# Rank-major place numbers with one load per unit, and overflow sums in bank 7 with three buffers of V

## The reference, cut to what matters

```python
h = relu(layernorm(x)); row, col = edge_index             # 6250 nodes, 206250 edges, float32
m = concatenate([h[col], edge_attr], axis=1)
m = relu(m @ W1.T + b1)
m = relu(m @ W2.T + b2)
summed = segment_sum(m, row, num_segments=6250)           # row = src, col = dst (sorted)
agg = summed / maximum(segment_sum(ones, row), 1)[:, None]
z = relu(concatenate([h, agg, u[batch]], axis=1) @ Wa.T + ba)
out = x + z @ Wb.T + bb
```

## Time and profile before

| | us |
|---|---|
| median of 3 runs | 1899.47 (1896.35 to 1899.72) |
| the profiled execution | 1902.48 |
| its span, first to last instruction | 1900.7 |
| first and last start of an indirect transfer on GpSimd | 69.6 and 1834.7 |

### The profile page before, as it was taken

The page is one execution under the profiler, slowest core; times in us unless marked ns, Lnnn a source line. Parts: engine busy times, 40 slices in busy tenths (PEclk is TensorE's granted clock), DMA queues, the critical chain, the costliest instruction groups (busy, mean ns, idle before and its releaser), DMA issues.

```text
span 1900.7 us, 43131 instructions
## 1 busy us (share of the span) xinstructions
PE 1732.0 (91%) x12376; PEld 1463.0 (77%) x12376; DVE 1340.0 (71%) x4868; ACT 1428.0 (75%) x2591; POOL 1509.7 (79%) x991
## 2 busy tenths in 40 slices
PE   5898888999999999999899999999999999976828
PEld 3676777888888888888788888888888888866725
DVE  8665655777777777778677777777777777755727
ACT  4687877888888888888788888888888888842315
POOL 8488888888888888888888888888888888878850
PEclk9999999999999999999999999999999999988968
DMA  9988888999999999999899999999999999997755
GB/s 330 269 169 145 156 148 141 199 197 205 195 207 187 199 203 199 194 205 197 176 199 194 199 202 200 195 194 209 202 191 201 200 204 202 199 210 155 159 136 198
DMA packets 312201, 369.10 MB, mean 194 GB/s; under 512 B 40832, under 2 KB 196064, under 8 KB 311328
## 3 DMA queue, kind: packets, MB, share of 16 engines
q1 hardware_dynamic: 175200, 302.12, 55.1%
q0 software_dynamic: 135360, 62.15, 34.5%
q10 hardware_dynamic: 1408, 2.03, 0.3%
HBM read 203.87 MB, written 159.27 MB: 191 GB/s over the span
## 4 chain that ended last, share of the span: by engine, by line
POOL 53%; issue 20%; DMA 11%; PE 9%; ACT 3%; DVE 2%; SPq 1%; POOLq 0%; ACTq 0%; DVEq 0%
POOL sums L819 48%; DMA sums<-regA,idx 9%; POOL sums L807 5%; PE bank L1351 2%; PE bank L1400 2%; PE bank L1362 1%; DMA sums<-vscat,vidx 1%; PE bank L1374 1%; ACT h L921 1%; PE bank L1390 1%; ACT regA L929 1%; PE bank L1276 1%; PE bank L1476 1%; ACT regA L955 0%; DMA p_table<-regB 0%
## 5 line engine op out<-in xcount | busy, mean ns | idle before, releaser
L819 POOL DMA_INDIRECT sums<-regA,idx x844 | 1318.3, 1562 | 293.0 <-issue 242.6
L1351 PEld LDWEIGHTS bank<-h,regC 128*128 128x128 f32 x3072 | 387.4, 193 | 180.7 <-ACT h L940 127.8
L1351 PE MATMUL bank<-h,regC 128*128 128x130 f32 x3072 | 432.0, 284 | 64.5 <-ACT h L940 64.5
L1374 PE MATMUL bank<-regA,L 128*128 128x512 f32 x806 | 432.3, 619 | 2.8 <-DVE regA L1143 2.7
L1400 PE MATMUL bank<-w,h 128*128 128x128 f32 x3224 | 430.1, 277 | 0.0
L1400 PEld LDWEIGHTS bank<-w,h 128*128 128x128 f32 x3224 | 396.8, 194 | 1.1 <-ACT h L921 0.6
L921 ACT ACTIVATE h<-bank,b1c 128x512 f32<-128x512 f32 x403 | 275.6, 684 | 136.9 <-PE bank L1374 131.9
L1362 PE MATMUL bank<-regC 128*128 128x129 f32 x2352 | 296.9, 280 | 23.0 <-DVE regB L1130 12.7
L1390 PEld LDWEIGHTS bank<-h,regC 128*128 128x128 f32 x1688 | 218.9, 191 | 119.7 <-issue 91.3
L1362 PEld LDWEIGHTS bank<-regC 128*128 128x128 f32 x2352 | 277.4, 194 | 37.3 <-ACT vscat L961 21.9
L904 ACT ACTIVATE regC<-bank 128x520 f32<-128x520 f32 x384 | 231.8, 604 | 87.8 <-PE bank L1351 84.5
(11 more groups left out here) (143 smaller groups left out, 1526.9 us busy)
## 6 DMA issues: line engine op xcount, KB each, us to landing
regC<-slots SPq DMA_DIRECT2D x294, 260.0 KB, 5.6
regA<-in_ea SPq DMA_DIRECT2D x202, 256.0 KB
slots<-regC SPq DMA_DIRECT2D x192, 260.0 KB
src<-rows_src SPq DMA_DIRECT2D x107, 256.0 KB
slots<-regC SPq DMA_DIRECT2D x192, 138.1 KB
sums<-regA,idx POOLq DMA_INDIRECT x844
dstR<-rows_dst SPq DMA_DIRECT2D x101, 128.0 KB
sums<-zeros SPq DMA_DIRECT2D x20, 645.0 KB, 6.7
```

Of the source, the lines that this page charges most:

```text
L819: nc.gpsimd.indirect_dma_start(out=sums[k], out_offset=bass.IndirectOffsetOnAxis(ap=idx[:, n % RING, t:t + 1], axis=0), in_=scat[:, n % 4, ...
L1351: last = T.matmul(psSlot(t)[:, k, :], place, h2[:, g % 2, t, :], start=True, stop=True)
L1374: T.matmul(psL1(s % 2), L[:, s % RING, :], R[:, s % RING, :], start=True, stop=True).then_inc(l1_done, 1)
```

## The change

Places are numbered rank by rank instead of bin by bin: place `j * 49 + b` is rank `j` of bin `b`, before it was `4 * b + j`. The permutation is built with its two inner loops exchanged (same 784 elements). The two bins of a unit now lie beside each other in `slots` for each rank, so that one DMA of 128 partitions with 4160 contiguous bytes replaces two with 2080 each. `arrived` counts one landing per load.

The overflow sums move from bank 1 to columns 260 to 388 of bank 7, beside the plain sums. V gets three buffers, and the waits before its first half is written are loosened by one pair. `VSUM` becomes 9 and `VLAG` 8: TensorE sums V in the step after, ahead of the plain sums of the same step, behind `free_sums`, and without the waits of L1422 and L1423; the unit's wait of L1426 goes; a wait for the overflow copy enters `free_sums` of a plain group, ahead of the next group's sums. ScalarE copies the overflow sums right behind the plain sums, not at the end of the step. GpSimd issues L807 three steps later, between two plain groups. With `VSUM` the last block's units shift: four instead of three of them run one to a step, and the last comes one step later.

```diff
-QLAG, VPRE, VREAD, VBC, VMASK, VSUM, VLAG = 6, 3, 7, 6, 7, 8, 5
+QLAG, VPRE, VREAD, VBC, VMASK, VSUM, VLAG = 6, 3, 7, 6, 7, 9, 8
 def arrived(m):
-    parts = {n: unit_bins(q)[1] for (_, q), n in UNIT_NO.items()}
-    return sum(parts[n] for n in users(m))
+    return len(users(m))
-        V = sb("V", [P, 2, W], f32)
+        V = sb("V", [P, 3, W], f32)
-        psVsum = bank[:, 1, PAIR * C:(PAIR + 1) * C]
+        psVsum = bank[:, 7, 2 * W:2 * W + C]
@@ sync: the unit's load
-                    for i in range(nb):
-                        sp.dma_start(loaded(m)[0:CAP * len(block), i, :, :].rearrange("p t c -> p (t c)"),
-                                     slots[h0:h0 + len(block), CAP * (b + i):CAP * (b + i + 1), :]).then_inc(unit_in[buffer_of(m)], 16)
+                    side_by_side = slots[h0:h0 + len(block), :, :].rearrange("n (j b) x -> (n j) (b x)", b=NBIN)
+                    sp.dma_start(loaded(m)[0:CAP * len(block), 0:nb, :, :].rearrange("p b t c -> p (b t c)"),
+                                 side_by_side[:, b * TPG * W:(b + nb) * TPG * W]).then_inc(unit_in[buffer_of(m)], 16)
@@ scalar: these lines move from the end of the step to behind the copy of the plain sums
+                if closes(s - VSUM):
+                    j = BINNED_NO[s - VSUM] // 2
+                    act.wait_ge(vsum_done, j + 1)
+                    if j >= 4:
+                        landed(act, BINNED[2 * (j - 4) + 1], 0)
+                    nc.scalar.activation(vscat[:, j % 4, :], psVsum, ACT.Copy).then_inc(vscat_ready, 1)
@@ vector
-                    VE.tensor_tensor(perm[:, n % 2, :, OVER:PW].rearrange("p t (b j) -> p t b j", j=CAP), ranked.unsqueeze(3).broadcast_to([P, TPG, NBIN, CAP]),
-                                     ranks[:, :].unsqueeze(1).unsqueeze(1).broadcast_to([P, TPG, NBIN, CAP]), ALU.is_equal).then_inc(perm_ready, 1)
+                    VE.tensor_tensor(perm[:, n % 2, :, OVER:PW].rearrange("p t (j b) -> p t j b", b=NBIN), ranked.unsqueeze(2).broadcast_to([P, TPG, CAP, NBIN]),
+                                     ranks[:, :].unsqueeze(1).unsqueeze(3).broadcast_to([P, TPG, CAP, NBIN]), ALU.is_equal).then_inc(perm_ready, 1)
-                        wait(dve, vsum_done, j - 1)
-                        wait(dve, vidx_ready, j - 1)
+                        wait(dve, vsum_done, j - 2)
+                        wait(dve, vidx_ready, j - 2)
@@ tensor: free_sums, and the sum of V ahead of the plain sums
                     pe.wait_ge(scat_ready, PLAIN_NO[g] + 1)
+                    wait(pe, vscat_ready, sum(1 for q in BINNED if closes(q) and q + VSUM <= g + 2))
+                if closes(s - VSUM):
+                    j = BINNED_NO[s - VSUM] // 2
+                    pe.wait_ge(vmask_ready, j + 1)
+                    free_sums(min(g - 1, NG - 1))
+                    T.matmul(psVsum, vS[:, j % 2, :] if not general else zeros[:, 0:P], V[:, j % 3, 0:C], start=True, stop=True).then_inc(vsum_done, 1)
-                if closes(s - VSUM):
-                    j = BINNED_NO[s - VSUM] // 2
-                    pe.wait_ge(vmask_ready, j + 1)
-                    wait(pe, vscat_ready, j)
-                    wait(pe, acc_ready, units_until(s - 1))
-                    T.matmul(psVsum, vS[:, j % 2, :] if not general else zeros[:, 0:P], V[:, j % 2, 0:C], start=True, stop=True).then_inc(vsum_done, 1)
                 for k, q in UNITS_AT.get(s, ()):
-                    wait(pe, vscat_ready, sum(1 for g in BINNED if closes(g) and g <= s - VSUM))
                     add_up(k, q, general)
```

More of the change, by code:

```diff
@@ L177, in added_for @@
     return m if m <= PAIRED else m - 1
-def units_until(s):
-    return sum(len(u) for at, u in UNITS_AT.items() if at <= s)
 def arrived(m):
-    parts = {n: unit_bins(q)[1] for (_, q), n in UNIT_NO.items()}
-    return sum(parts[n] for n in users(m))
+    return len(users(m))
 def unit_bins(q):
@@ L612, in _ @@
                     sp.wait_ge(vpre_ready, 2 * j + 2)
-                    sp.dma_start(V[OVER:2 * OVER, j % 2, :], vpre[:, :]).then_inc(v_in[j % 2], 16)
+                    sp.dma_start(V[OVER:2 * OVER, j % 3, :], vpre[:, :]).then_inc(v_in[j % 2], 16)
                 for k, q in LOADS_AT.get(s, ()):
@@ L1165, in _ @@
                     wait(dve, vsum_done, j - 1)
-                    VE.scalar_tensor_tensor(out=vS[:, j % 2, :], in0=psVrow, scalar=V[:, j % 2, C:W], in1=tri[:, :],
+                    VE.scalar_tensor_tensor(out=vS[:, j % 2, :], in0=psVrow, scalar=V[:, j % 3, C:W], in1=tri[:, :],
                                             op0=ALU.is_equal, op1=ALU.mult, accum_out=vcnt[:, j % 2:j % 2 + 1]).then_inc(vmask_ready, 1)
@@ L1194, in _ @@
                     wait(dve, vscat_ready, j - 1)
-                    VE.tensor_tensor(vidx[:, j % 6:j % 6 + 1], vextra[:, j % 2:j % 2 + 1], V[:, j % 2, C:W], ALU.max).then_inc(vidx_ready, 1)
+                    VE.tensor_tensor(vidx[:, j % 6:j % 6 + 1], vextra[:, j % 2:j % 2 + 1], V[:, j % 3, C:W], ALU.max).then_inc(vidx_ready, 1)
                 if is_sorted(s - VPRE):
@@ L1205, in _ @@
                     link(VE.tensor_tensor(vhalf[:, :, :], slot_sb[0:OVER, n % 2, 0, 0:2, :], slot_sb[0:OVER, n % 2, 0, 2:4, :], ALU.add))
-                    VE.tensor_tensor(V[0:OVER, j % 2, :] if half == 0 else vpre[:, :], vhalf[:, 0, :], vhalf[:, 1, :], ALU.add).then_inc(vpre_ready, 1)
+                    VE.tensor_tensor(V[0:OVER, j % 3, :] if half == 0 else vpre[:, :], vhalf[:, 0, :], vhalf[:, 1, :], ALU.add).then_inc(vpre_ready, 1)
                 for k, q in UNITS_AT.get(s - 1, ()):
@@ L1410, in step @@
                     wait(pe, overslot_ready, sum(1 for g in BINNED if g <= s))
-                    T.transpose(psVrow, V[:, j % 2, C:W].broadcast_to([P, P]), ident[:, :]).then_inc(vrow_done, 1)
+                    T.transpose(psVrow, V[:, j % 3, C:W].broadcast_to([P, P]), ident[:, :]).then_inc(vrow_done, 1)
                 if is_sorted(s + 2):
```

## The result

The changed kernel takes 1908.22 us (median of 6, 1906.69 to 1910.23), the kernel before beside it 1897.95 us (1895.25 to 1899.72): ratio 1.0056, 95% interval 1.0044 to 1.0068, some 10 us slower. The profiled execution took 1908.03 us, span 1906.2.

The account below looks back on a forecast made before the run. GpSimd's 940 indirect transfers, 1.850 us each, were taken to bound the kernel. 69.6 + 1765.1 - 2.6 + 66.0 = 1898.1 us of span, 1899.9 profiled, 3.0 above the median, gave 1896.9 us; range 1889.5 to 1904.5.

Parts of the forecast that it names:

- What bounds the kernel: GpSimd's middle stretch: 940 transfers at 1.850 us back to back; changes outside GpSimd could win at most 28 us there.
- always more than four transfers of work: GpSimd's queue: read from the copies' leads, 8.5 us or more for overflow groups, so other engines' waits were covered.
- The slack: ScalarE's wait at L929 for `scat` buffers, 62.3 us before, was to grow toward 90 us as TensorE gets further ahead.
- The overflow lead: Time from the overflow copy's end to GpSimd taking it: from about 8.5 us to some 25 us, worth 0.
- R4: Rival: VectorE's new permutation holds GpSimd's transfers up 192 times, 154 us, time 2054 us; chance 0.03.
- One load per unit: SP's loads: 144 fewer DMAs relieve GpSimd's landings, -2.6 us together, bounds 0 and -10.5 us.
- The sum: Whole kernel: start, GpSimd's stretch, -2.6 us and end give 1898.1 us of span, median 1896.9 us, 0.14% below before.
- a line through two mean packets: DMA engines: packets of 93 and 155 ns gave 0.030 ns a byte plus 43 ns a packet, saving 42 us each.
- How does DMA share turn into stops?: GpSimd's landing stops: 10 points of DMA share cost 4.7 us, so 3 points return 1.6 us, plus 1.0 at the end.
- R3: Rival on the 16 DMA engines: longer load packets ahead of GpSimd's scatters delay landings, +11 us, 1910 us; chance 0.12.

## Why the prediction was wrong

**What bounds the kernel: right.** GpSimd's transfers take 1.545 us with a gap of 236.8 / 777 = 0.305 in the changed kernel too, 940 of them, and the time moved with the last of them. One reading was too wide: "always more than four transfers of work" holds for the copies, but `idx` leads its transfer by only 5.6 us in the last steps of the kernel before, three transfers. The spacing there ran into that.

**The overflow sums: right.** Worth 0, shown by the run that changes them alone (1.0007). The wait of the earlier trace rows is gone; the units' line L1358 idles for this instead:

```profile
  DVE regB L1125: 7.1, 6
  issue: 7.0, 5
```

The slack turned up where it was forecast, at the `scat` buffers, but more of it: 121.3 + 18.4 = 139.7 us, forecast about 90, before 62.3.

```profile
ACT regA L924 <- DMA sums<-regA,idx: 121.3, 40, 9.1
...
ACT regA L924 <- DMA sums<-vscat,vidx: 18.4, 10, 9.7
```

The overflow lead grew from 8.5 us to 29.2 (forecast 25): the copy at 1049.27 + 0.28 is taken at 1078.79.

```profile
1049.27 0.28 ACT L930 ACTIVATE vscat<-bank 128x129 f32<-128x129 f32 x1
...
1078.79 1.54 POOL L802 DMA_INDIRECT sums<-vscat,vidx  x1 [0.30 <-issue]
```

**The permutation: right**, 963 ns for 962; R4 did not happen.

**One load per unit: wrong in sign.** The sum had it at -2.6 us; alone it costs 0.69%, some 13 us, and in the changed kernel 10. Two steps failed.

The first is the size of what is saved. I drew a line through two mean packets and took 43 ns a packet, 3 points of the engines' share. In the 680 us from 1000 on, 8871 packets fewer and the same bytes took 56.4% for 57.6%: 1.2 points, 0.012 x 16 x 680 / 8871 = 15 ns a packet. The row from the tables' loads had other traffic around it and carried the slope.

The second step made the error: "How does DMA share turn into stops?" It took the average share of a stretch as the cause. Its 10 points came from the unit loads' presence, and the removal of packets was to give a third of that back. The share did fall, 0.95 to 0.93, and the middle stretch gave nothing back: 7.6 us of stops above the gap for 7.5, where -1.6 was forecast. In the last block, where -1.0 was forecast, they rose by 5.3. The runs point to what lies in SP's queue when a transfer is issued, and the change doubles what SP hands over in one issue. The view that would have shown it was SP's queue by time in the last block: four loads took 2.48 us to issue. I had the issue time of one load before me and counted its halving as nothing, since SP was not the bound.

**R3** had the right place (the DMA engines), the right sign and, by luck, the price (+11 us; measured +10), at a chance of 0.12. It spread the harm over all 150 loads, with over 50 stops; there are 44. Its mechanism was the longer packet, and that is refuted: short runs in one DMA lose 0.58%, long runs in two lose nothing. I had misread the rule that I quoted from the Trainium skill (DMA: Bandwidth & Descriptors, Queues, rings and completion order), by taking the packet of that page for one row of a load. The page gives a packet as some 9 to 17 descriptors, 64 at most. The windows without a packet of GpSimd's hold 258 and 426 of the profile's packets, 16 and 27 for each of the 16 engines: if a descriptor is one of these, both are within the page's limit, the second above its usual size. By bytes, 0.82 MB is 51 KB an engine, more than the 33 KB of a whole unit load. What unit the engines take turns in, no row here shows.

**What stays open.** That GpSimd's packets stay out for up to 4.7 us while two 520 KB loads are in the queue is seen in the records, and that spacing them mends the changed kernel is measured. Whether it is the bytes waiting in the queue or something in a single large DMA is not told apart: in these kernels the bytes of one DMA and the pace of SP's issue go together. Nor is it only the engines' time: in the window with short runs they were busy 73.6%, and still no packet of GpSimd's came. The two loads spaced don't decide it, since VectorE's `idx` hides what the landings gave back. Nor is it settled what the 125 loads before the last block cost: 0.36% on the kernel before, 0.20% left with the last block spaced, and nothing that can be measured on the changed kernel with it. Of the 5.5 us that the profiles show, the last block has 5.0 of excess.

## What to carry to other kernels

When an engine is paced by transfers that must land within a few microseconds, judge another queue's traffic by how much is handed over at once in the busiest stretch, not by the average share of the DMA engines. Joining DMAs saves the engines little (15 ns a packet here) and can double the burst; if they are joined, wait for one to land before the next is issued, and check that the engines which need the loads have slack left for that wait: it undid the loss in the changed kernel and gave nothing where `idx` led by 5.6 us. And look for a long instruction of another engine beside the pacing one: moving one gave 0.24% on the kernel before, though nothing that can be measured on the changed one.

## What the runs showed of the hardware

- GpSimd's indirect transfers got no packet through for 4 us while SP's queue held two 520 KB loads and one of 256 KB (258 packets, 0.82 MB, 96.0% of the engines).
- SP issued a 520 KB load in as little as 0.32 us (changed kernel, median 0.51), and one of 260 KB of the kernel before in 0.60 us in the median. Rank-major addresses alone brought that to 0.48.
- An indirect transfer beside VectorE's 3.48 us addition of two on-chip operands took 3.4 to 4.6 us, ending 1.42 us after it where it had begun beside its start, and 1.54 us in the median otherwise.
- Loading 64 partitions at a time cost 0.48% where they were neighbours (1.0048) and nothing that can be measured where they were every second one (1.0005).
